# A two-layer transformer stack on one core: two of eight MoE tiles are issued in halves between the score and value blocks on TensorE

## The reference

```python
x = _layernorm(x + _L0_attn_ref(...))  # linear attention over channels: Gram-like products, 256x256 matrices
x = _layernorm(x + _L0_ffn_ref(...))   # MoE: out += weights[:, e] * (x @ expert_w[e] + b[e]) for 8 experts
x = _layernorm(x + _L1_attn_ref(...))  # softmax over the 16 heads of one token; scores 16x16 per token
x = _layernorm(x + _L1_ffn_ref(...))   # router, the best 768 of 1024 rows get gelu(x @ w_block)
```

## Time and profile before

| | us |
|---|---|
| median of 3 runs (lowest, highest) | 1730.85 (1727.42, 1743.65) |
| the profiled execution | 1728.09 |
| its span, first to last instruction | 1726.3 |
| PE busy | 1283.3 (74%) |
| DVE busy | 1017.2 (59%) |
| POOL busy | 627.6 (36%) |
| ACT busy | 551.2 (32%) |
| mean granted TensorE clock | 0.817 |

### The profile page before, as it was taken

One profiled execution on the slowest core, in us unless ns is written; L12 is line 12 of the kernel. 1 busy time (PEld: TensorE's weight loads), 2 busy tenths in 40 slices (PEclk: granted clock), 3 DMA queues, 4 the chain that ended last, 5 costly groups with the idle time before them and its releaser, 6 DMA issues. The chain is left out here.

```text
span 1726.3 us, 33300 instructions
## 1 busy us (share of the span) xinstructions
PE 1283.3 (74%) x12232; PEld 805.2 (47%) x12232; DVE 1017.2 (59%) x2249; ACT 551.2 (32%) x1100; POOL 627.6 (36%) x890
## 2 busy tenths in 40 slices
PE   0768977798688977698678978698778978585342
PEld 0444545545464544555364545555364545442341
DVE  2142556476664856477573857477573858475635
ACT  2022332235223442136223352136223351144113
POOL 3113335134442355135352355135352355044212
PEclk9879987799868897699778987699778987598566
DMA  3000072203701073101801063201801062206220
GB/s 127 13 13 1 0 131 42 50 1 71 127 2 49 1 146 53 50 1 57 141 2 50 1 128 71 50 1 53 145 2 50 1 122 50 50 1 127 45 50 25
DMA packets 92912, 90.69 MB, mean 53 GB/s; under 512 B 7031, under 2 KB 81721, under 8 KB 92474
## 3 DMA queue, kind: packets, MB, share of 16 engines
q1 hardware_dynamic: 90170, 79.93, 23.6%
q0 software_dynamic: 2560, 8.39, 1.5%
HBM read 46.35 MB, written 41.94 MB: 51 GB/s over the span
## 5 line engine op out<-in xcount | busy, mean ns | idle before, releaser
L1412 PE MATMUL bank<-we,at 128*128 128x512 f16 x1536 | 387.7, 415 | 39.2 <-issue 16.3
L1412 PEld LDWEIGHTS bank<-we,at 128*128 128x128 f16 x1536 | 158.4, 106 | 249.9 <-issue 79.3
L512 POOL TENSOR_TENSOR part<-part 128x512 f32<-128x512 f32 x64 | 83.5, 1305 | 394.6 <-ACTq L790 394.6
L973 DVE TENSOR_TENSOR stage<-bank,stage 128x512 f16<-128x512 f32 x128 | 87.5, 688 | 187.1 <-ACT stage L654 187.0
L654 ACT ACTIVATE part<-bank,wexp 128x256 f32<-128x256 f32 x256 | 105.8, 470 | 250.6 <-PE bank L1412 217.1
L1412 PE MATMUL bank<-bt,wqkv 128*128 128x512 f16 x576 | 156.5, 419 | 25.9 <-DVE stage L973 23.9
L1128 DVE SCALAR_TENSOR_TENSOR x<-bank,wexp,x 128x256 f32<-128x256 f32 x256 | 122.8, 480 | 60.9 <-PE bank L1412 46.9
L766 ACT ACTIVATE x<-x,nm,rs 128x256 f32<-128x256 f32 x192 | 104.6, 593 | 142.3 <-POOL nm L500 141.1
L654 ACT ACTIVATE stage<-bank 128x512 f16<-128x512 f32 x128 | 76.3, 597 | 218.5 <-PE bank L1412 160.3
L493 POOL TENSOR_SCALAR nm<-mv 128x2 f32<-128x2 f32 x128 | 29.7, 232 | 279.6 <-DVE mv L1005 275.5
L1422 PE MATMUL bank<-const,x 128*128 128x128 f32 x384 | 63.1, 293 | 72.4 <-ACT x L766 72.3
(11 more groups left out here) (176 smaller groups left out, 2279.1 us busy)
## 6 DMA issues: line engine op xcount, KB each, us to landing
scratch_qkv<-stage SPq DMA_DIRECT2D x48, 512.0 KB, 6.7
ct<-scratch_qkv SPq DMA_DIRECT2D x128, 128.0 KB, 5.4
x_in<-in_x_dram SPq DMA_DIRECT2D x32, 256.0 KB, 4.9
keys<-scratch_qkv SPq DMA_DIRECT2D x64, 128.0 KB, 6.0
scratch_o<-stage SPq DMA_DIRECT2D x64, 128.0 KB, 3.1
bt<-scratch_o SPq DMA_DIRECT2D x16, 512.0 KB, 3.7
out_dram<-x POOLq DMA_DIRECT2D x32, 256.0 KB, 2.7
blockdiag<-in_expert_w_dram SPq DMA_DIRECT2D x1, 2048.0 KB
```

Source lines behind the costliest of these rows:

```text
L512: pool.tensor_tensor(part[:, 0:2, :], part[:, 0:2, :], part[:, 2:4, :], ALU.add)\
L973: return dve.tensor_tensor(dst, src, hi, ALU.subtract)
L1412: ins = pe.matmul(dst, lhs, rhs, start=(n == 0), stop=(n == len(terms) - 1))
```

## The change

Only PE's order is changed. `a_moe` gets an argument that names the quarters to issue. Quarters 0 and 1 of moe2 now stand between S0 and S1, and quarters 2 and 3 between S1 and PT0. Quarters 0 and 1 of moe3 stand between O0 and O1, and quarters 2 and 3 between O1 and O2; behind `a_srow` no MoE tile is left. DVE, ACT, POOL and SP keep their orders, and no instruction is added or taken away.

```diff
-            def a_moe(a, t):
-                for q in range(4):
+            def a_moe(a, t, quarters=range(4)):
+                for q in quarters:
...
                     b_s(c, 0)
+                if b is not None:
+                    a_moe(b, 2, range(2))
+                if c is not None:
                     b_s(c, 1)
                 if b is not None:
-                    a_moe(b, 2)
+                    a_moe(b, 2, range(2, 4))
...
                     b_o(c, 0)
+                if b is not None:
+                    a_moe(b, 3, range(2))
+                if c is not None:
                     b_o(c, 1)
+                if b is not None:
+                    a_moe(b, 3, range(2, 4))
+                if c is not None:
                     b_o(c, 2)
                     b_o(c, 3)
                 if a is not None:
                     a_srow(a)
-                if b is not None:
-                    a_moe(b, 3)
```

## The result

The kernel got slower. The forecast was 1787. The profiled execution took 1790.53 us at a mean granted clock of 0.818 (0.817 before), so the clock as a whole is not what changed.

A forecast was written before the change was run, and what follows sets the result against it. The DRAM trip for bt from O3 to PR0, 14 to 15 us, was taken to bound the kernel, hiding moe3. 1728.1 + 55 (moe3) + 3 (score blocks) = 1786, or 1789 from the median; forecast 1787, range 1766 to 1808.

The forecast's parts named there:

- What bounds the turn: From O3 to PR0: the DRAM trip for bt takes 14 to 15 us; work ahead of O3's end adds one to one.
- The rival that PR0 does not set the turn: At PR0: something else sets when the turn goes on, so no change, 1731 us; chance 0.04.
- Moe3's price: Value blocks: split moe3 costs 7.85 us a turn, 55 us over seven turns, bounds 37 and 74.
- The first half: Moe3 between O0 and O1: starts at half clock, loses 1.7 us, takes 4.35 us.
- the second half: Moe3 between O1 and O2: full clock 2.65 us or half again 4.35 us, middle taken, 3.5 us.
- the rival of full clock: Value and score blocks: clock stays full, moe3 costs 37 us, moe2 returns 6; 1759 or 1762 us; chance 0.12.
- the rival of half clock: Value and score blocks: moe3's halves too short for the clock to rise, 74 plus 12 us, 1814; chance 0.10.
- The score blocks: Moe2 split around S1: costs 3 us in all, bounds -13 and +12 us.
- The ninth turn: Score blocks: S1 stands behind moe2's wait for DVE, so S2 comes 3 us later.
- The six looped turns: Score blocks: delay taken as 0, upper bound 1.5 us a turn, worked out from the fourth turn.
- S1 on DVE: Score blocks: DVE late with S1 by 1 to 4 us, S2 not late except in the ninth turn.
- the bound of the gain: Score blocks: at best -1.8 us a turn, moe2 falling from 7.18 us to 5.34 at full clock, -13 us.

The follow-up runs named there:

- e2_value: Kernel before with only moe3 split: quarters 0 and 1 between O0 and O1, 2 and 3 between O1 and O2; 1780.45 us, ratio 1.026.
- e1_score: Kernel before with only moe2 split: quarters 0 and 1 between S0 and S1, 2 and 3 behind S1; 1751.06 us, ratio 1.0105.
- e9_before_again: The kernel before, unchanged, run again for a second profile; 1735.67 us, ratio 0.9998.
- e10_score_again: e1_score unchanged, run again for a second profile; 1754.55 us, ratio 1.0112 against the kernel before.
- e3_half: Kernel before with quarters 0 and 1 of moe3 between O0 and O1, quarters 2 and 3 left behind a_srow; 1766.3 us, ratio 1.0179.
- e5_dve_swap: Kernel before with one exchange on DVE: moe1's reads ahead of the second filling of blockdiag instead of behind it; 1751.52 us, ratio 1.0088.
- e7_moe3_ahead_O0: Kernel before with moe3 moved whole to ahead of O0, where PE waits for ct; 1739.99 us, ratio 1.0017.
- e11_score_spread: e1_score with DVE's second filling of blockdiag put ahead of moe0's reads; 1760.35 us, ratio 1.0141 against the kernel before.
- e4_moe4_early: Kernel before with MoE tile 4 brought forward on all four engines to right behind moe3; 1708.59 us, ratio 0.9837.

## Why the prediction was right, and where not

The time and the direction came out: 1795.6 for 1787, inside 1766 to 1808. The sum was nearer than its terms, because two errors have opposite signs.

- **What bounds the turn.** Right. Work put ahead of the end of O3 was paid one to one: half of moe3 costs 28 us in the stretch and 31 in the time, all of it 46 and 45, and moe3 ahead of O0, in a wait, costs 2 us, which its interval can't tell from none. The trip stayed at 14 us, and the wait at PR0 went to 111.5 us for a forecast of 110. The rival that PR0 does not set the turn has fallen.
- **Moe3's price: 55 us forecast, 42 to 46 measured.** The first half was about right (4.35 us forecast, 3.6 to 4.6 measured in the kernel after, 4.0 to 5.2 in e2_value). The term that was mis-sized is the second half, put at the middle of 2.65 and 4.35, 3.5 us: it took 2.6 to 2.75 us at full clock in every turn. Half of the rival of full clock came true with that, and the rival of half clock fell, though in three turns of e2_value the first half took 5.1 to 5.2 us, nearly the 5.3 of half clock. The 6 us that the rival of full clock hoped to get back from moe2 did not show in the time.
- **The Trainium skill's rule, TensorE: Matmul & The Clock Gate, section Why this matters for your kernels,** that matmuls without breaks bring the clock up: the trace agrees for the second halves of moe3 (granted clock 1.00, had 0.50 in the same blocks without moe3). For moe2 in e1_score it does not carry over S1 (0.65 and 0.56 in the second half of the fourth turn, with no idle time ahead of it). By the forecast's reading of the rule the mixing should have come out at the rival's 1759 to 1762, and the kernel took 1795.6: moe3 took 6.4 to 7.3 us, hardly less than the 7.04 before (6.7 to 8.0 in e2_value), and in its new place it cost some 6 us a turn where it had cost nothing.
- **The score blocks: 3 us forecast, 16 to 19 measured.** The ninth turn was as forecast: S0 to O0 is 3.0 to 3.7 us longer, the same as S1's 3.0. PE's wait for DVE at that place in the kernel after is 4.71 us (the earlier trace rows had 1.80), and S1 follows it:

```profile
1493.60 3.11 PE L1412 MATMUL bank<-keys,blockdiag 128*128 128x16 f16 x96
1501.42 5.30 PE L1412 MATMUL bank<-we,at 128*128 128x512 f16 x12 [4.71 <-DVE x L1128]
```

  The six looped turns cost nothing where DVE was as in the earlier trace rows, also as forecast. The step that failed is that I worked the looped turn out from one turn, the fourth, whose DVE was only a little late, and took it for all: "I take 0 for the six looped turns, with 1.5 us as the bound above". In 4 of 18 such turns the filling on DVE takes some 4 us longer or more, and the turn then costs 6 to 8 us. At 4/18 and some 7 us that is 9 us over six turns, of which an unsplit kernel pays about 4 (7/30 of its turns, at 3). The bound of 1.5 us was the error: it held for a wait of usual length, and the sum over the turns is made by the few long ones. That the sum came within 9 us of the time is partly luck: 9 to 13 us too much for moe3 stand against 13 to 16 too little for the score blocks.
- **What stays open.** Ninth turn and events make 3.4 + 5 = 8 to 9 us of the 16 to 19, by the mean frequency of events. The two profiles taken together, e9_before_again and e10_score_again, both within 2 us of the median of their runs, close better: their spans differ by 16.0 us, and S0 to O0 makes 13.4 of it, with two events. (e1_score's profile is the fastest of its six runs, 9 us below the median.)
- **The stretch that the change does not touch.** The profiles of the score split also show PR0 to the next S0 at 889.2, 891.2 and 893.5 us, where before has 884.1 and 884.6 and e2_value 882.1, so 5 to 11 us more. This stretch has the same work in the same order in all of them. It is not the later PR0 (e2_value has that too) nor the longer wait at PR0 (e1_score has 63.0 us of it, before 63.4). Nor does it need the split: e3_half, e5_dve_swap and e7_moe3_ahead_O0, without it, have 889.7, 889.1 and 890.5. In part it is the speed of the same matmuls: PE is busy in it for 731.9 us in before, 743.0 in after, and 741.5 and 740.8 in e3_half and e7_moe3_ahead_O0, but 734.8 in e1_score. No experiment tells what makes the rest.
- **S1 on DVE: late in most turns, but not in the one it was worked out for.** I had forecast S1 to come 1 to 4 us late on DVE in the looped turns. Counted from the start of S0, in the kernel after against before, it comes 4.1 us later in the third and fifth turn, 0.9 and 1.0 in the sixth and seventh, and 10.1 in the eighth, the event. In the fourth turn of the kernel after S0 starts at 478.85, and DVE takes up S1 at 487.56 and S2 at 495.20, so 8.7 and 16.3 us behind S0; before it was 8.7 and 18.2. DVE was not late there, and moe2 ran at full clock, in 5.5 us for 7.4. From the timeline of PE:

```profile
481.82 2.75 PE L1412 MATMUL bank<-we,at 128*128 128x512 f16 x12
484.40 3.12 PE L1412 MATMUL bank<-keys,blockdiag 128*128 128x16 f16 x96
487.36 2.76 PE L1412 MATMUL bank<-we,at 128*128 128x512 f16 x12
```

  S0 to O0 is 36.9 us in this turn for 38.7 before, so the 1.8 us that I had as the bound of the gain do come in this turn. They do not come in all: moe2 took 5.5 us in three of the six looped turns of the kernel after and in one of e1_score, and 7.2 us in three of e1_score, where S0 to O0 is 38.4 to 38.5 us; and one event of 7 us takes back four such gains.
- **Small things.** In the fifth turn O3 ends at 717.03 (706.62 + 10.41), not 716.9, so the trip there takes 14.2 us. The upper end of the range, 1808, starts from the median; from 1728.1, as the lower end, it would be 1806. The piece from O0 to O3 was announced at 17 to 21 us and is 16.1 to 17.0, the two halves at 7 to 9 us and are 6.4 to 7.3. DVE's idle time before L1194 was to stay near 12 us and grew to between 13.7 and 15.1, two microseconds for the 7 that PE's idle time grew.

## What to carry to other kernels

A wait for a trip through memory is a place for work, and its worth is its length: moving a 7 us tile out of it cost 6 us a turn, moving a second one in gained 3.8 (26.9 us over seven turns). Whether a chunk may stand between two blocks is asked of what it waits for: a block behind it inherits that wait, also at its worst, so its price is to be read from many turns of several profiles, the worst among them, not from one turn. And before an order of VectorE is changed, look at what POOL copies beside it; a swap of two steps that "moves nothing" cost 14 us.

## What the runs showed of the hardware

- A POOL copy of 128x2048 16-bit numbers (3.6 to 4.3 us) and a DVE tensor-scalar instruction of the same size (0.75 us alone) do not run beside each other: a DVE instruction that starts half a microsecond into the copy stretches to 4.1 to 4.4 us, and ends 0.55 us behind it. POOL's additions beside the filling are slower as well (1.71 us against 1.26 for L512, kernel after against e11_score_spread), and DVE's median instruction in the 13.3 us filling of the eighth turn is 1.43 us.
- Behind the first half of moe3 (3.6 to 5.2 us) and 2.6 us of 16-column matmuls the second half ran at full clock in 7 of 7 turns of after and of e2_value. Behind the first half of moe2 and the 3.1 us of S1 it often did not: 4.4 us for the second half in five of seven turns of e1_score. So the first observation is no rule.
- At PR0 the clock starts at half level after a long quiet, and takes some us of busy PE to rise. Windows of PE at PR0, fifth turn (fourth in the last), first of the kernel before (6.9 us of idle time ahead of it):

```profile
731.30:734.30 3.00, 3.00 (x15) 0.50 0.00 0
734.30:737.30 3.00, 3.00 (x28) 0.97 0.00 0
```

  then of the kernel after (13.7 us):

```profile
750.60:753.60 3.00, 2.98 (x15) 0.50 0.00 0
753.60:756.60 3.00, 3.00 (x18) 0.58 0.00 0
756.60:759.60 3.00, 3.00 (x30) 1.00 0.00 0
```

  and of e4_moe4_early (1.3 us):

```profile
527.50:530.50 3.00, 2.97 (x28) 1.00 0.00 0
```

  Whether a longer quiet makes the rise slower is not shown. Over the seven turns the clock is full 3.0 to 5.0 us behind PR0 in the kernel before and 4.0 to 6.0 in the kernel after, but 3.0 to 5.5 in e2_value, whose quiet is as long; in e4_moe4_early it is full from the start in all seven. The 128x256 matmuls of PR0 to PR3 take 337 ns on average after, 318 before, 325 in e9_before_again and in e2_value, and 282 in e4_moe4_early. In e7_moe3_ahead_O0 they take 337 too, at 2.3 us in the whole time, so this is small.
- The blocks of 16-column matmuls gain next to nothing from the clock: in the kernel after, 102 of them meet the first 2.5 us of O2 at a granted clock of 1.00, and 97 to 100 every 2.5 us of the value blocks at 0.50 in the kernel before. All four blocks took 10.11 us behind moe3 at full clock in e7_moe3_ahead_O0, and 10.41 us in the earlier trace rows.
